# Attention chunk sums in f16 parts, their value stage in the ring of first scores, and halves in four-step turns

## The reference

```python
x = x + _L0_conv_ref(_gn(x), ...)          # 7x7 window attention with 4 heads, and an MLP
t = _to_tokens(x)                          # 16 x 3136 x 32
t = t + _L1_attn_ref(_ln_t(t), Wq, bq, Wk, bk, Wv, bv)
t = t + _L1_ffn_ref(_ln_t(t), ...)         # 16 experts, each takes its 8 best tokens

def _L1_attn_ref(x, ...):
    q, k, v = x @ Wq + bq, x @ Wk + bk, x @ Wv + bv
    scores = einsum('bqd,bkd->bqk', q, k) / sqrt(d)
    return einsum('bqk,bkd->bqd', softmax(scores), v) + x
```

## Time and profile before

| what | us |
|---|---|
| median of 3 runs (2839.5 to 2844.89) | 2842.47 |
| profiled execution, its own time | 2842.57 |
| its span, first to last instruction | 2840.8 |
| TensorE matmul busy | 2696.5 (95%) |
| VectorE busy | 2365.5 (83%) |
| ScalarE busy | 2053.3 (72%) |
| GpSimd busy | 621.7 (22%) |

### The profile page before, as it was taken

The page is one execution under the profiler, slowest core; times in us unless marked ns, Lnnn a source line. Parts: engine busy times, 40 slices in busy tenths (PEclk is TensorE's granted clock), DMA queues, the critical chain, the costliest instruction groups (busy, mean ns, idle before and its releaser), DMA issues.

```text
span 2840.8 us, 62058 instructions
## 1 busy us (share of the span) xinstructions
PE 2696.5 (95%) x25297; PEld 1286.0 (45%) x25297; DVE 2365.5 (83%) x4335; ACT 2053.3 (72%) x3927; POOL 621.7 (22%) x506
## 2 busy tenths in 40 slices
PE   4899999999689999999999999999999999999987
PEld 3455555555343444444444444444444444444447
DVE  4899999999378888888888888888888888888834
ACT  4688888888546777777777777777777777777762
POOL 0566666666101010110101101011011010110100
PEclk6899999999889999999999999999999999999997
DMA  3000000000390101011010110101101001010003
GB/s 99 7 19 25 25 19 25 19 25 19 141 292 1 24 1 24 1 24 24 1 24 1 24 24 1 24 1 24 24 1 24 14 11 24 1 24 1 1 1 92
DMA packets 92592, 82.30 MB, mean 29 GB/s; under 512 B 61109, under 2 KB 82198, under 8 KB 91286
## 3 DMA queue, kind: packets, MB, share of 16 engines
q1 hardware_dynamic: 92085, 78.29, 10.6%
q10 hardware_dynamic: 224, 0.07, 0.0%
HBM read 39.60 MB, written 32.11 MB: 25 GB/s over the span
## 4 chain that ended last, share of the span: by engine, by line
PE 84%; DVE 6%; ACT 5%; issue 1%; DMA 1%; SPq 1%; POOL 0%; POOLq 0%; DVEq 0%; ACTq 0%
PE ps L1697 22%; PE ps L1648 20%; PE ps L1674 19%; PE ps L1707 3%; PE ps L1478 3%; DVE arena L1142 3%; PE ps L1497 2%; PE ps L1470 2%; PE ps L1488 2%; PE ps L1509 2%; DVE arena L1251 2%; ACT arena L726 1%; PE ps L1754 1%; PE ps L1525 1%; PE ps L1548 1%
## 5 line engine op out<-in xcount | busy, mean ns | idle before, releaser
L1251 DVE TENSOR_REDUCE arena<-ps 128x1 f32<-128x448 f32 x2800 | 1544.1, 614 | 244.7 <-PE ps L1648 244.7
L894 ACT ACTIVATE arena<-ps 128x512 f32<-128x512 f32 (+1 forms) x2464 | 1249.9, 606 | 369.1 <-PE ps L1674 369.0
L1648 PE MATMUL ps<-arena 96*128 96x448 f16 x2800 | 999.5, 358 | 14.1 <-DVE arena L1243 8.6
L1674 PE MATMUL ps<-arena 97*128 97x512 f16 x2800 | 937.6, 355 | 2.9 <-ACT arena L894 1.6
L1697 PE MATMUL ps<-arena 128*32 128x512 f32 (+2 forms) x7328 | 671.2, 457 | 0.7 <-DVE arena L1273 0.7
L1674 PEld LDWEIGHTS ps<-arena 97*128 97x128 f16 x2800 | 259.4, 100 | 411.2 <-ACT arena L894 295.6
L1697 PEld LDWEIGHTS ps<-arena 128*32 128x32 f32 x7328 | 252.1, 109 | 390.3 <-ACT arena L894 204.5
L1648 PEld LDWEIGHTS ps<-arena 96*128 96x128 f16 x2800 | 274.6, 98 | 285.3 <-DVE arena L1251 114.0
L624 POOL TENSOR_TENSOR tok<-arena,tok 128x128 f32<-128x128 f32 (+1 forms) x112 | 47.7, 426 | 1514.0 <-DVE arena L1273 1514.0
L569 POOL TENSOR_TENSOR arena<-arena 113x784 f32<-113x784 f32 x128 | 192.7, 1505 | 156.5 <-DVE arena L1118 156.5
L564 POOL TENSOR_TENSOR arena<-arena 113x784 f32<-113x784 f32 x128 | 192.6, 1505 | 86.0 <-DVE arena L1107 85.9
(11 more groups left out here) (184 smaller groups left out, 2530.4 us busy)
## 6 DMA issues: line engine op xcount, KB each, us to landing
arena<-qk_scratch SPq DMA_DIRECT2D x96, 196.0 KB, 4.0
qk_scratch<-arena SPq DMA_DIRECT2D x16, 448.0 KB, 5.2
arena<-ximg SPq DMA_DIRECT2D x16, 400.0 KB, 6.9
arena<-in_x SPq DMA_DIRECT2D x4, 1568.0 KB, 11.4
xa_scratch<-arena SPq DMA_DIRECT2D x32, 196.0 KB, 1.9
res_scratch<-arena SPq DMA_DIRECT2D x32, 196.0 KB, 2.0
arena<-xa_scratch SPq DMA_DIRECT2D x4, 1568.0 KB, 9.9
arena<-res_scratch SPq DMA_DIRECT2D x4, 1568.0 KB, 13.8
```

Of the source, the lines that this page charges most:

```text
L894: act.activation(pk[0:rows, x % DEPTH, QC * m:QC * m + n], ps[0:rows, w % SB, 0:n], ACT.Exp, scale=float(C) ** -0.5).then_inc(att["exp"], 1)
L1251: dve.tensor_reduce(mxp[0:rows, p, u:u + 1], ps[0:rows, MB + j % RB, 0:KN], AX_X, ALU.max)\
L1648: pe.matmul(ps[:, MB + j % RB, 0:KN], q2[p][0:96, T * t:T * t + T], k2[p][0:96, KN * m:KN * m + KN], start=True, stop=True).then_inc(att[" ...
L1674: last = pe.matmul(ps[:, bank, at_ % QC:at_ % QC + chunk_cols(c)], k2[p][0:97, T * t:T * t + T], q2[p][0:97, QC * c:QC * c + chunk_cols(c) ...
```

## The change

Several things change together. A third step is cut into halves in four-step turns too. GpSimd splits a chunk's sums into an f16 high part `uh` and an f16 rest `ul` (in the space of small weights that are no longer needed), and the value weights are kept as f16 parts `wvh` and `wvl`, made once in the setup. The value stage is three f16 matmuls per tile instead of one f32 matmul. It comes one turn later (`OUT_LATE` = 3 turns after the chunk's last turn, behind two first scores and one second score), and it takes a bank of the ring, as one more use in the ring's order. Key sums wait for ScalarE's copy, not for the division. `bank_of` and `bank_user` work out which bank each use has and whose end it must wait for.

```diff
+        wvh = sb("wvh", [128, C + 1], F16)
+        wvl = sb("wvl", [128, C + 1], F16)
-        OUT_AT = 5
+        OUT_AT, OUT_LATE = 3, 3
+        ring = [(what, i) for k in range(NTURN) for what, i in turn_steps(k) if what != "second"]
+        bank_of = {use: n % RB for n, use in enumerate(ring)}
+        bank_of.update({("out", (NQ - 2, 0)): 2, ("out", (NQ - 1, 0)): 3})
+            def split_sums(b, c):
+                n = chunk_cols(c)
+                pool.wait_ge(att["acopy"], b * NQ + c + 1)
+                if not (isinstance(b, int) and b * NQ + c == 0):
+                    pool.wait_ge(att["out"], b * NQ + c)
+                pool.tensor_copy(uh[:, 0:n], ua[:, 0:n]).then_inc(att["ahigh"], 1)
+                pool.wait_ge(att["ahigh"], b * NQ + c + 1)
+                pool.tensor_tensor(ul[:, 0:n], ua[:, 0:n], uh[:, 0:n], ALU.subtract).then_inc(att["alow"], 1)
...
                     for c, late in chunk_ended(k - 2):
                         if not (late and first):
+                            split_sums(b - late, c)
+                    for c, late in chunk_ended(k - OUT_LATE):
+                        if not (late and first):
                             tokens(b - late, (p + late) % 2, c)
...
+            split_sums(B - 1, NQ - 2)
             tokens(B - 1, 1, NQ - 2)
+            split_sums(B - 1, NQ - 1)
             tokens(B - 1, 1, NQ - 1)
...
@@ sums_copy @@
+                if not (isinstance(b, int) and b * NQ + c == 0):
+                    act.wait_ge(att["alow"], b * NQ + c)
...
-            dve.tensor_copy(wvo[:, :], ps[:, ZB, 320:321 + C])
+            step(dve.tensor_copy(wvh[:, :], ps[:, ZB, 320:321 + C]))
+            dve.tensor_tensor(wvl[:, :], ps[:, ZB, 320:321 + C], wvh[:, :], ALU.subtract)
-                o4 = ps[0:rows, AVB, 0:(C + 1) * k].rearrange("p (t n) -> p t n", n=C + 1)
+                o4 = ps[0:rows, MB + m, 0:(C + 1) * k].rearrange("p (t n) -> p t n", n=C + 1)
...
@@ key_sums @@
-                    pe.wait_ge(att["o"], b * NQ + c)
+                    pe.wait_ge(att["acopy"], b * NQ + c)
-                alone = full and (len(turn_of) == 3 and x == turn_of[2])
+                alone = full and turn_of.index(x) == 2
...
-            def out_values(b, c):
+            def out_values(b, c, m):
-                pe.wait_ge(att["acopy"], b * NQ + c + 1)
+                pe.wait_ge(att["alow"], b * NQ + c + 1)
                 for q in chunk_tiles(c):
                     i = q % 4
-                    last = pe.matmul(ps[:, AVB, (C + 1) * i:(C + 1) * (i + 1)], ua[:, T * i:T * i + T], wvo[:, :],
-                                     start=True, stop=True)
+                    for part, w in ((uh, wvh), (uh, wvl), (ul, wvh)):
+                        last = pe.matmul(ps[:, MB + m, (C + 1) * i:(C + 1) * (i + 1)], part[:, T * i:T * i + T], w[:, :],
+                                         start=(part is uh and w is wvh), stop=(part is ul))
                 last.then_inc(att["out"], 1)
...
+            def wait_for_bank(b, use, first=False, last=False):
+                what, i, back = bank_user(use, first, last)
+                if what == "ahead":
+                    pe.wait_ge(att["ring"], i + 1)
+                elif what == "first":
+                    pe.wait_ge(att["ring"], (b - back) * NJ + AHEAD + i + 1)
+                else:
+                    c, late = i
+                    pe.wait_ge(att["o"], (b - back - late) * NQ + c + 1)
...
-            out_values(B - 1, NQ - 2)
             for x in turns[-1]:
                 key_sums(B - 1, 1, x, True)
-            out_values(B - 1, NQ - 1)
+            for c in (NQ - 2, NQ - 1):
+                wait_for_bank(B - 1, ("out", (c, 0)), last=True)
+                out_values(B - 1, c, bank_of["out", (c, 0)])
...
@@ token_columns, experts @@
+                if f == 1:
+                    pe.wait_ge(att["o"], B * NQ)
```

More of the change, by code:

```diff
@@ L50 @@
 VS_CG = 14
-VS_STAGE0 = 16
+VS_STAGE0 = 17
 XN = 4
@@ L138, in conv_attention_moe @@
         wvb = sb("wvb", [C + 1, C + 1])
-        wvo = sb("wvo", [128, C + 1])
+        wvh = sb("wvh", [128, C + 1], F16)
+        wvl = sb("wvl", [128, C + 1], F16)
         gateb = sb("gateb", [128, 1])
@@ L202, in conv_attention_moe @@
         ua = carve(QC)
+        spare = wsmall[:, :, :, :].rearrange("p i j c -> p (i j c)")
+        uh, ul = (spare[:, QC // 2 * i:QC // 2 * (i + 1)].bitcast(F16) for i in range(2))
         rden = carve(8)
@@ L265, in conv_attention_moe @@
             "load0", "load1", "score1", "ring", "maxall", "mrow", "score2", "exp",
-            "av", "acopy", "out", "rden", "o", "tok", "sum", "mean", "diff", "square", "ss", "var", "rstd", "xf")}
+            "av", "acopy", "ahigh", "alow", "out", "rden", "o", "tok", "sum", "mean", "diff", "square", "ss", "var", "rstd", "xf")}
         moe = {n: sem("moe_" + n) for n in (
@@ L376, in conv_attention_moe, with turn_steps, bank_user @@
         assert all(turns[k][-1] < (first_of + [NSTEP])[c] for k, c in row_turn.items()) and len(row_turn) == NQ
+        def turn_steps(k, last=False):
+            for what, i in turn_order(k, last):
+                if what == "out":
+                    for c, late in chunk_ended(k - OUT_LATE):
+                        yield what, (c, late)
+                else:
+                    yield what, i
+        ring = [(what, i) for k in range(NTURN) for what, i in turn_steps(k) if what != "second"]
+        bank_of = {use: n % RB for n, use in enumerate(ring)}
+        bank_of.update({("out", (NQ - 2, 0)): 2, ("out", (NQ - 1, 0)): 3})
+        def bank_user(use, first=False, last=False):
+            m = bank_of[use]
+            before = [("ahead", u, u % RB) for u in range(AHEAD)] if first else [(*x, bank_of[x]) for x in ring]
+            own = [(*x, bank_of[x]) for x in ring if not (first and x[0] == "out" and x[1][1])
+                   and not (last and x[0] == "first" and jobs[x[1]][0])]
+            own += [("out", (c, 0), bank_of["out", (c, 0)]) for c in range(NQ) if last and ("out", (c, 0)) not in ring]
+            n = [x[:2] for x in own].index(use)
+            back = 0
+            for line, back in ((own[:n], 0), (before, 1)):
+                users = [x for x in line if x[2] == m]
+                if users:
+                    return users[-1][0], users[-1][1], back
+            raise ValueError(use)
         SB, AVB = 3, 3
@@ L653, in image_steps @@
                         if not (late and first):
+                            split_sums(b - late, c)
+                    for c, late in chunk_ended(k - OUT_LATE):
+                        if not (late and first):
                             tokens(b - late, (p + late) % 2, c)
-                    for what, j in turn_order(k):
+                    for what, j in turn_steps(k):
                         if what == "first" and j == LN_AT + 4:
@@ L1244, in _, with consume @@
             last.then_inc(s_clear2, 1)
-            def consume(b, p, u, j, done):
+            def consume(b, p, u, m, done):
                 t = u // NK
@@ L1250, in consume @@
                 dve.wait_ge(att["score1"], done)
-                dve.tensor_reduce(mxp[0:rows, p, u:u + 1], ps[0:rows, MB + j % RB, 0:KN], AX_X, ALU.max)\
+                dve.tensor_reduce(mxp[0:rows, p, u:u + 1], ps[0:rows, MB + m, 0:KN], AX_X, ALU.max)\
                    .then_inc(att["ring"], 1)
@@ L1260, in consume, with weighted @@
                                       AX_X, ALU.max).then_inc(att["maxall"], 1)
-            def weighted(b, p, c):
+            def weighted(b, p, c, m):
                 k, rows = len(chunk_tiles(c)), tile_rows(4 * c)
                 i = (NQ * p + c) % 2
-                o4 = ps[0:rows, AVB, 0:(C + 1) * k].rearrange("p (t n) -> p t n", n=C + 1)
+                o4 = ps[0:rows, MB + m, 0:(C + 1) * k].rearrange("p (t n) -> p t n", n=C + 1)
                 dve.wait_ge(att["out"], b * NQ + c + 1)
@@ L1300, in image_steps @@
                 for k in range(NTURN):
-                    for what, j in turn_order(k, last):
+                    for what, j in turn_steps(k, last):
                         if what == "out":
-                            for c, late in chunk_ended(k - 2):
-                                if not (late and first):
-                                    weighted(b - late, (p + late) % 2, c)
+                            c, late = j
+                            if not (late and first):
+                                weighted(b - late, (p + late) % 2, c, bank_of[what, j])
                         if what == "first":
                             ahead, u = jobs[j]
-                            consume(b + ahead, (p + ahead) % 2, u, j, b * NJ + AHEAD + j + 1)
+                            consume(b + ahead, (p + ahead) % 2, u, bank_of[what, j], b * NJ + AHEAD + j + 1)
                             if j == LN_AT:
@@ L1318, in _ @@
             for u in range(AHEAD):
-                consume(0, 0, u, u, u + 1)
```

(28 more changed lines are left out.)

1 line of the change is left out of this document (added).

## The result

The changed kernel takes 2770.95 us (median of 4 runs, 2766.62 to 2772.38) against 2841.78 before (median of 4); the ratio is 0.9747, 95% interval 0.9731 to 0.9764: some 71 us faster. The forecast was 2762 us, range 2746 to 2798. The profiled execution took 2770.49 us, 72.1 less than the one of before.

A forecast was written before the change was run, and what follows sets the result against it. The prediction took TensorE to bound the attention images. Its terms, 41.3 + 43.2 + 1.8 - 4.2 - 0.9 - 0.2 = 81.0 us, taken from 2842.6 gave 2762 us, range 2746 to 2798.

The forecast's parts named there:

- TensorE bounds the attention: Sixteen attention images: TensorE busy 116.56 of 116.90 us, so TensorE time removed is time gained if VectorE and ScalarE keep up.
- Part 1: Key sums behind four-step turns: halving the third step saves 0.43 us, 96 times, 41.3 us.
- the sums need nothing sooner: Key sums with halves: nothing they need must come sooner; ScalarE makes the last probabilities well inside the turn.
- Part 2: Value stage in f16: 0.35 us instead of 0.80 per full chunk, 43.2 us, plus 1.8 us for one-tile chunks.
- 0.18 us by columns alone: Value stage, low end: if only columns count, twelve f16 matmuls take 33/64 of 0.35 us.
- the load rule: Value stage, loads rival: 107 ns per 128-column load, 1.28 us for twelve, 46 us lost, 2851 us; chance 0.05.
- Part 3: Value stage one turn later in the ring: free in ordinary turns, 0.6 us wait in the norm's turn, loss 4.2 us.
- 0.14 us of VectorE idle time: End of the turn receiving the value stage: VectorE idle time left from 0.22 us, so TensorE still ends it.
- Part 4: GpSimd's split per chunk: two operations of 1.07 us, some 2.4 with hand-offs, 1.5 us spare, so hidden.
- Part 5: Once, outside the steady stretch: splits after the last image cost 0.9 us, setup 0.2 us.
- the ring binds: Rival: the ring of banks stalls TensorE 0.34 us in every chunk, 33 us, giving 2795 us; chance 0.10.
- late split: Rival: TensorE waits at the value stage for GpSimd's low part, 73 us slower than before, 2915 us; chance 0.06.

The follow-up runs named there:

- e9: Changed kernel with the row of maxima behind the second step in two turns and the norm's square sum behind a later turn's last reduce: 2752.08 us.
- e1: Kernel before with only the halves in four-step turns added: 2816.61 us, ratio 0.9909.
- e2: Changed kernel without the halves in four-step turns: 2800.92 us, ratio 0.9857.
- e3: Changed kernel with the row of maxima put behind the second step instead of the first, twice an image: 2761.36 us.
- e4: Changed kernel with one f32 value matmul per tile and no GpSimd split, stage still one turn later in the ring: 2810.38 us.
- e6: Changed kernel with the value stage two turns after a chunk's last turn instead of three, in the split's turn: 3122.98 us.

## Why the prediction was right, step by step

- *TensorE bounds the attention*: right, before and after, and e9 closes nearly all that was left of its idle time.
- *Part 1, the halves, 41.3 us*: the step that was mis-sized. By the turns it is (1.64 + 0.15 - 0.08) x 16 = 27.4 us; e1 and e2 measured 23.7 and 30.0, and 28 in the images. The 0.43 a turn was right for four turns of six (0.41). I multiplied by six without looking at what else stood in each turn. In two, a row of maxima lies among the sums. While the third step used two of four column groups, the row's matmuls and its wait for ScalarE cost nothing, and halving took that cover away: e2 shows it there (2.06 with a row and without), e3 prices the wait at 8.2 us in the images. My sentence that the sums need nothing sooner overlooked the row. The trace of the kernel before had a sign of it, which I didn't read. In turns 3, 7, 11, 15 and 19 a row stands among the sums of a three-step turn, whose third step was halved already. There the row starts after 0.06 us, hardly waits, and the sums still take 1345.77 - 1344.10 = 1.67 us, where those without a row take 1.43. TensorE's timeline before:

```profile
1344.10 0.62 PE L1697 MATMUL ps<-arena 128*32 128x512 f32 x2
1344.16 0.22 PE L1659 MATMUL ps<-negid,mq 128*1 128x128 f16 x1
...
1345.77 0.36 PE L1648 MATMUL ps<-arena 96*128 96x448 f16 x1
```

- *Part 2, the f16 value matmuls, 43.2 + 1.8 us*: right in kind. 25 ns per matmul was measured for the 29 taken from the row of 64 columns, so 0.30 us for 0.35 between first and second score. By whole turns the stage took 0.75 and now takes 0.23, a saving of 0.52 where 0.45 was forecast. But it saves this in five chunks of six, since in the norm's turn it saves nothing. So it is partly luck that 41.8 us, the format's gain by e4, is near 45.0. The Trainium skill, "TensorE: Matmul & The Clock Gate", in its part on why 56 ns and not 53.3, puts the least distance of two matmul starts near 25 ns, however few columns; this trace agrees, and neither 15 ns (the prediction's 0.18 us by columns alone) nor 107 ns by the load rule came true.
- *Part 3, the move*: right in an ordinary turn, where TensorE waits for nothing. The 0.14 us of VectorE idle time was only roughly right: behind turns 1, 6 and 22 it is 0.26 to 0.39, behind 14 and 18 there is none (under 0.1 us), and TensorE doesn't wait even there. In the norm's turn the wait was 0.40 for 0.6. For the move the sum had a loss of 4.2 us; e4, which makes it with f32 matmuls, gained 5.3 over e1, because the norm's turn takes in a stage of 0.80 us for 0.41. Parts 2 and 3 together were 40.8 us in the sum and 2.98 x 16 = 47.7 in the trace (the last three lines of the table).
- *Part 4, the split*: right that it is hidden; 1.85 us for 2.4, since the copy takes 0.61, not 1.07 (the subtraction 1.16), and 1.6 to 2.3 us spare for 1.5. The reduces stayed at 604 to 627 ns.
- *Part 5, the ends, 1.1 us*: too small. 72.1 - 27.4 - 47.7 leaves a loss of 3.0 us; this compares one profiled execution of each kernel. From the first key sums to the token transposes behind the last image the changed kernel is 74.2 us faster, 0.9 less than the turns' 75.1: that is what was forecast for the splits in the chain. Behind it 1.8 us are lost from the transposes to GpSimd's power, and 2.4 from there to the end; ahead of the first key sums 2.2 are gained. The 1.8 us come from the clock, which the prediction left out: 16 transposes take 3.66 us (at 2657.73), where they took 2.84 before (at 2734.08), and the four matmuls behind them 1.98 for 1.08. The first fence is TensorE's timeline of the end, with its two waits for the split. The second has the windows view of the transposes' stretch, after and then before, with granted clocks of 0.50 (1.2 GHz) and 0.67: the clock was partly down before too.

```profile
2655.40 0.18 PE L1756 MATMUL ps<-wvh,wsmall 128*128 128x33 f16 x1 [0.96 <-POOL wsmall L666]
...
2657.64 0.19 PE L1756 MATMUL ps<-wvh,wsmall 128*128 128x33 f16 x1 [1.79 <-POOL wsmall L666]
...
2657.73 3.66 PE L1869 MATMUL ps<-cst,ximg 128*128 128x128 f32 x16
```

```profile
2657.70:2661.50 3.80, 3.80 (x21) 3.47 (x23) 1.39 (x5) 1.19 (x2) 0.24 (x1) 0.50 0.00 0
...
2734.08:2736.90 2.82, 2.82 (x17) 2.62 (x18) 1.07 (x4) 0.98 (x2) 0.25 (x1) 0.67 0.00 0
```

That the waits for the split lowered it is likely, but not shown. e1 has no split, and its transposes take 3.44 us; e9 has it, and they take 3.01. In e4, without a split and with waits of 0.81 and 0.65 us, they take 1.94 at a clock of 1.00, in its timeline and windows view:

```profile
2700.29 0.94 PE L1729 MATMUL ps<-arena 128*32 128x64 f32 x50 [0.81 <-ACT arena L915]
...
2702.89 0.38 PE L1740 MATMUL ps<-wvo,wsmall 128*128 128x33 f32 x2 [0.65 <-issue]
2703.11 1.94 PE L1854 MATMUL ps<-cst,ximg 128*128 128x128 f32 x16
```

```profile
2703.11:2705.05 1.94, 1.94 (x18) 1.73 (x18) 1.07 (x4) 1.00 (x2) 0.47 (x2) 1.00 0.00 0
```

So the terms were off by -13.9, +6.9 and -1.9, which makes the 8.9 us between 81.0 and 72.1: the forecast came as near as it did because the second error made up for half of the first, which is luck. Of the rivals none came true: the ring binds in one turn of an image, not in every chunk. The late split's price was too low, as e6 shows.

What stays open: the stretch from the first of the expert stage's GpSimd powers on (at 2745.0 us before, at 2670.5 after) lasts 95.8 us before and 98.2 after, and 96.9 to 100.5 in e1 to e9, two of which have no split (e1 96.9, e4 97.7). So the split isn't shown to be its cause, and it may be no more than what differs between executions; that wasn't followed up. No kernel was run that takes the split out of the end alone.

## What to carry to other kernels

Before a saving is multiplied by its count, list what else stands in each place: an idle part of an engine may be covering somebody else, and filling it brings that into the open. With a ring of buffers, an engine's idle time at a turn's end says nothing of its slack in the middle; a long operation belongs behind the last job that the ring waits for. A stage that is paid for in a turn where its engine waits anyway costs less than it lasts, and saves less when it is made shorter.

## What the runs showed of the hardware that was not expected

A pause of 2.0 us in an otherwise full TensorE can halve its clock for the rest of a turn: e6 lost 352 us over 96 full chunks, 3.7 us each with the one-tile chunks counted in, against some 2 us of waiting, and not every such pause did it (9.68 and 6.63 us for two turns with the same wait). What decides it stays open. And f32 matmuls that leave two of four column groups idle hid four f16 matmuls and a wait of 0.3 us completely.
